# A fused vision block on one core: attention's value product on 64x32 tiles instead of 113x64 block-diagonal stationaries, and one filler left out

## The chip, the cores and the metric

The kernel runs on one core of a Trainium2 chip. The metric is the device time of one execution in microseconds, in float32 but for two small MLPs. Before: 3321.04 us, the median of three runs (3319.8 to 3326.78).

## The reference

The input x is 32 images of 56x56 tokens with 24 channels. Five layers follow each other; the change touches the first:

```python
# L0: shifted window attention, 7x7 windows, 3 heads of 8 channels, then an MLP
shifted = roll(x, (-3, -3)); win = window_partition(shifted)      # 32*64 windows of 49 tokens
h = layernorm(win); q, k, v = h @ wq, h @ wk, h @ wv              # 24 -> 3 heads x 8
attn = softmax(q @ k.T / sqrt(8) + mask)                          # per head, 49x49
out = (attn @ v).reshape(-1, 49, 24) @ wo + bo
t = x + window_reverse(out); t = t + gelu(layernorm(t) @ w1 + b1) @ w2 + b2
# L1: layernorm, 24 -> 48, 3x3 convolution back to 24, silu, residual
# L2, L3: per channel a Fourier mixer over the 3136 tokens, then an MLP in fp8, both with residuals
```

The value product is `attn @ v`; the change computes the same sums.

## The kernel before, in words

**Layout.** Four images are worked on together, a "quad": image j has its channels on partitions 32j to 32j+31 (24 channels, some constants), its tokens along the free axis. `for q in range(nq)` runs eight quads one after the other: window_attention, mlp, conv, then twice mixer and ffn. Each engine has its own program, written out by hand in this order; semaphores (`wait_ge`, `then_inc`) join them. All matrix products go through `mm` at L1128, so every one of them has that line in the profile, and is told apart by its tiles and shape. A float32 product is recorded as two passes, each a weight load (PEld) and a matmul (PE).

**Window attention** (L1213). A quad has 8 rows of 8 windows. One step n works on two windows of four images; there are 32 steps, four to a row of windows (t = n // 4, dw = n % 4). The loop is a software pipeline, and TensorE's queue in each iteration is:

- scores of the step 6 ahead (8 products, 32 partitions by 49 columns) and turned scores of this step (8 products). They wait for `maxed`, which VectorE's row maximum (L979) of the step before releases, and for `exped`, ScalarE's exponential (L741) of the step before.
- the value product of the step before (L1283 to L1291): for 2 windows, 3 heads and 2 pairs of images, one product of `ring` (stationary) and `pt` (moving). `ring` holds the values of a pair of images as a block diagonal: image 2g on partitions 64 to 112 in columns 0 to 31, image 2g+1 on partitions 0 to 48 in columns 32 to 63, and a column of ones by which the softmax sum comes out. The three heads are added up in bank 4 of PSUM. The last one releases `weighed`.
- at dw = 0 keys and queries (`wk`, `wq`) of two rows of windows ahead; at dw = 1 the sums spread over the channels (`spread`) with the centering of the second norm, then the values of the next row (`xh`, `wv`: 16 products, 128 partitions by 49 columns) and a transpose of the row maxima; at dw = 3 the output projection with the variance.

ScalarE copies keys (L755) and queries (L762, two halves) out of PSUM, takes exponentials (L741), squares and logarithms of the norms (L707, L719, L724) and the output (L747). VectorE takes maxima (L979), writes value blocks (L1009), multiplies keys and queries by head masks (L996, L1019), adds the residual (L987) and divides by the softmax sum (L1028).

**MLP** (L1353). `MLP_ORDER` starts with row 0, whose norm is ready. After its first product TensorE's queue has at i = 1 the filler `keep_busy(4, 1)` (L1359): one product of constants, 128x128 by 448 columns, into bank 4, whose result nobody reads. Then the last row's centering (L1363), its variance (L1365), and `keep_busy(5, 2)`; after that, rows 7, 1, 2 and so on. ScalarE loads the table of gelu (L794, 1.28 us) once its last root of the norm (L724) is done, and takes gelu of every half row; the convolution's first table load (L799) ends the stage for it. `keep_busy` stands in six other places, which stay.

**GpSimd** builds a table for the mixer before the first quad's part of it (L593 to L601, products and stores in turn), and only then zeroes borders and copies rows from `xw` to `xs` (L642), for which the convolution's centering waits.

Of the kernel before, what the change touches and what calls it, by code (L numbers as in the profile page):

```python
# [23 lines left out]
QI = 4  # L24
NQ = B // QI
RW = 32
WS, SHIFT, NH, DH = 7, 3, 3, 8
L = WS * WS
# [16 lines left out]
PADL = 64  # L45
STEPS = NW * NW // 2
SIDE = PADL + L
# [84 lines left out]
def ln_count(q, k):  # L132

    return q * LN_N + NW + k + 1
# [66 lines left out]
def down_bank(i):  # L201

    return 6 + (i + 1) % 2
# [61 lines left out]
def build_kernel(nc, x, keep, raw, g2, g4, out, nq=NQ):  # L265
    ctx = ExitStack()
    with ctx:
# [42 lines left out]
        ps = ctx.enter_context(nc.psum_tensor("ps", [128, 8, 512], F32))  # L310

        def K(name):
            at, n = KEEP_AT[name]
            return keep_sb[:, at:at + n]
# [7 lines left out]
        def part(area, at, *shape):  # L322
            n = int(np.prod(shape))
            v = area[:, at:at + n]
            if len(shape) == 2:
                v = v.rearrange("p (a b) -> p a b", b=shape[1])
            if len(shape) == 3:
                v = v.rearrange("p (a b c) -> p a b c", b=shape[1], c=shape[2])
            return v, at + n

        at = 0
        km, at = part(area_h, at, 2, NW, NH * L)
        qk, at = part(area_h, NTOK, 5, NW, PADL)
        qs, ks = qk[:, 0:2], qk[:, 2:5]
        mx, at = part(area_h, at, 2, 2 * NW * NH)
        mxt, at = part(area_h, at, 2, SIDE)
        assert at <= 2 * NTOK
        qm, at = part(area_t, 0, 3, NW, NH * L)
        pt, at = part(area_t, at, 2, 2, 6 * L)
        assert at <= HW * PAIR  # L340
        osb, at = part(area_y, 0, 2, TW)
        osn, at = part(area_y, at, 2, TW)
        lns, at = part(area_y, at, TW)
        rec, at = part(area_y, at, TW)
        assert at <= NTOK
        ring = area_z.rearrange("p (b u n) -> p b u n", b=2, n=NH * PADL)
# [11 lines left out]
        yc, at = [None, None], 0  # L358
# [15 lines left out]
        m29, at = part(area_t, 0, QI * CI)  # L374
        down, at = part(area_t, at, 2, 2 * RW)
        yy = area_h[:, 0:2 * NTOK].rearrange("p (g n) -> p g n", g=2)
        xq8 = area_t[:, 0:NTOK // 4].bitcast(F8)
        at = NTOK // 4
# [747 lines left out]
        def _(pe):  # L1126
            def mm(o, a, b, start=True, stop=True):
                return pe.matmul(o, a, b, start=start, stop=stop)  # L1128
# [9 lines left out]
            def crossed(bank, w, still, moving):  # L1138

                for o in range(0, 128, BLOCK):  # L1140
                    r = slice(o, o + BLOCK)
                    ins = mm(ps[BLOCK - o:2 * BLOCK - o, bank, 0:w], still[r, r], moving[r, :])
                return ins
# [24 lines left out]
            def keep_busy(bank, n):  # L1168

                for _ in range(n):  # L1170
                    mm(ps[:, bank, 0:TT], K("center"), keep_sb[:, 0:TT])
# [41 lines left out]
            def window_attention(q):  # L1213
# [25 lines left out]
                for n in range(-8, STEPS + 4):  # L1239
                    t, dw = n // 4, n % 4  # L1240
                    k = n + AHEAD
                    u = k // 4
# [31 lines left out]
                    k = n - 1  # L1274
                    if 0 <= k < STEPS:

                        u = k // 4
                        pe.wait_ge(exped, q * STEPS + k + 1)
                        if k % 4 == 0:
                            pe.wait_ge(v_kept, q * NW + u + 1)  # L1280
                            if u >= 1:
                                pe.wait_ge(out_kept, q * NW + u)
                        for i in range(2):  # L1283
                            w = 2 * (k % 4) + i
                            for h in range(NH):
                                for g in range(2):
                                    o = NH * L * i + L * h
                                    ins = mm(ps[PADL * g:PADL * g + PADL, 4, L * w:L * w + L],
                                             ring[0:SIDE, u % 2, 2 * w + g, PADL * h:PADL * h + PADL],
                                             pt[0:SIDE, k % 2, g, o:o + L], start=h == 0, stop=h == NH - 1)  # L1290
                        ins.then_inc(weighed, 1)  # L1291
                    if dw == 0 and 1 <= t + 2 < NW:

                        u = t + 2
# [10 lines left out]
                    if dw == 1 and 0 <= t - 1 < NW:  # L1305
# [5 lines left out]
                        if t - 2 >= 0:  # L1311
# [4 lines left out]
                            i = t - 2  # L1316
# [5 lines left out]
                    if dw == 1 and 0 <= t + 1 < NW:  # L1322

                        u = t + 1
                        pe.wait_ge(k_kept, q * NW + min(u + 2, NW))
                        for w in range(NW):
                            for jj in range(2):
                                far = PADL - PADL * jj
                                ins = mm(ps[far:far + L, 7, 2 * C * w:2 * C * w + 2 * C],
                                         xh[:, TW * u + L * w:TW * u + L * w + L], wv[:, jj, :])  # L1330
# [7 lines left out]
                    if dw == 3 and 0 <= t - 1 < NW:  # L1338
# [3 lines left out]
                        if t - 2 >= 0:  # L1342
                            k = LN_AT[LN_WIN2, t - 2]
# [9 lines left out]
            def mlp(q):  # L1353
                pe.wait_ge(w2_loaded, 16 * HC)
                for i in range(NW + 1):
                    if i < NW:
                        row = MLP_ORDER[i]
                        if i == 1:
                            keep_busy(4, 1)  # L1359
                            pe.wait_ge(attended, q * NW + NW)  # L1360
                            pe.wait_ge(logged, ln_count(q, LN_AT[LN_WIN2, NW - 2]))
                            k = LN_AT[LN_WIN2, NW - 1]
                            crossed(6, TW, K("center"), xw[:, TW * (NW - 1):TW * NW]).then_inc(centered, 1)  # L1363
                            pe.wait_ge(squared, ln_count(q, k))
                            crossed(6, TW, K("variance"), sq[:, k % 2, 0:TW]).then_inc(var_made, 1)  # L1365
                            keep_busy(5, 2)
                        pe.wait_ge(normed, ln_count(q, LN_AT[LN_WIN2, row]))
                        for p in range(2):
                            u = 2 * i + p
                            if u >= 3:  # L1370
                                pe.wait_ge(geglu, q * 2 * NW + u - 2)
                            pe.sem_inc(passed_pe, 1)
                            for jj in range(2):
                                r = slice(64 * p + RW * jj, 64 * p + RW * jj + RW)
                                ins = mm(ps[0:HID, 2 * (u % 3) + jj, 0:TW], w1[r, :],
                                         xh[r, TW * row:TW * row + TW])
                            ins.then_inc(up_made, 1)
                    if i >= 1:
                        i1 = i - 1
                        if i1 >= 2:  # L1380
                            pe.wait_ge(mlp_added, q * NW + i1 - 1)
                        pe.wait_ge(geglu, q * 2 * NW + 2 * i1 + 2)
                        pe.sem_inc(passed_pe, 1)
                        for j in range(QI):
                            ins = mm(ps[RW * j:RW * j + RW, down_bank(i1), 0:TW], w2[:, :],
                                     hid[0:HID, (2 * i1 + j // 2) % 4, j % 2, :])
                        ins.then_inc(down_made, 1)
# [265 lines left out]
            for q in range(nq):  # L1653
                window_attention(q)
                mlp(q)
                conv(q)
                for l in range(2):
                    mixer(q, l)
                    ffn(q, l)
# [168 lines left out]
```

## Time and profile before

| | |
|---|---|
| median of three runs | 3321.04 us |
| profiled execution, its own time | 3324.36 us |
| its span | 3322.6 us |
| mean granted TensorE clock | 0.971 of full |
| TensorE busy, weight loads busy | 87%, 55% |
| VectorE, ScalarE, GpSimd busy | 50%, 48%, 11% |
| chain of work that ended last | TensorE 69%, ScalarE 13%, VectorE 7%, issue 7% |

The span is the time from the first to the last instruction, the execution's own time is 1.8 us more. The chain of waits is followed back from the last instruction; "issue" is time in which an engine waited for nothing that the profile shows. Ends of matmuls are modelled, so the start of a matmul or of a weight load says more than its end. Times in the rows are microseconds from the start of the span.

### The profile page before, as it was taken

Reading aid. Unit: us, or ns where it says so; the run is one execution under the profiler, and the core shown is the slowest. Engines: PE = TensorE matmul, PEld = TensorE weight load, DVE = VectorE, ACT = ScalarE, POOL = GpSimd, SP = SyncE. Lnnn points to the kernel's source line nnn. Section 1 sums busy time; section 2 is a strip of 40 time slices with the busy share of each in tenths; the row PEclk is TensorE's granted clock in tenths of the full one; section 3 lists DMA queues with packets and bytes.
Section 4 is the critical chain, followed back from the end, with each engine's and each line's share of the span. In section 5 each row is a group of like instructions: output and inputs, shape, how many; then the busy total and the mean of one; then the engine's idle time right before and its main releaser. Section 6 shows DMA issues by size and latency. Waiting matters only on the chain.

```text
span 3322.6 us, 110007 instructions
## 1 busy us (share of the span) xinstructions
PE 2898.2 (87%) x49148; PEld 1838.1 (55%) x49148; DVE 1665.9 (50%) x2707; ACT 1611.3 (48%) x2899; POOL 363.6 (11%) x574
## 2 busy tenths in 40 slices
PE   6868889888899898998989989888898988988888
PEld 3536546466455573564744747447465474553754
DVE  5524546355553545544464445644457354572554
ACT  3542455533555425644266353563535535456245
POOL 4520010000100011001010011000110001100001
PEclk8989999999999999999999999999999999999999
DMA  2322000210001100110001100021000210001100
GB/s 80 69 59 52 2 16 5 53 33 2 17 16 50 25 2 17 32 51 6 2 18 42 46 1 2 18 54 34 1 2 19 54 34 1 2 19 34 33 1 16
DMA packets 28434, 84.79 MB, mean 26 GB/s; under 512 B 22002, under 2 KB 23138, under 8 KB 24114
## 3 DMA queue, kind: packets, MB, share of 16 engines
q1 hardware_dynamic: 26690, 72.55, 9.1%
q8 instruction: 395, 6.47, 0.8%
q0 software_dynamic: 1280, 5.21, 0.6%
q14 instruction: 69, 0.57, 0.1%
HBM read 61.70 MB, written 14.84 MB: 23 GB/s over the span
## 4 chain that ended last, share of the span: by engine, by line
PE 69%; ACT 13%; DVE 7%; issue 7%; SPq 3%; DMA 1%; ACTq 0%; DVEq 0%
PE ps L1128 69%; ACT lv L719 2%; SPq L495 2%; ACT area_ty L851 2%; ACT rs L724 2%; ACT sq L707 1%; DMA area_hz<-f_all 1%; DVE xs L1098 1%; DVE area_hz L979 1%; ACT area_hz L762 1%; ACT sq L705 1%; ACT area_ty L843 1%; DVE area_hz L996 1%; DVE area_ty L1094 1%; DVE area_ty L1070 1%
## 5 line engine op out<-in xcount | busy, mean ns | idle before, releaser
L1128 PE MATMUL ps<-area_hz 32*49 32x147 f32 (+3 forms) x7180 | 363.7, 288 | 89.2 <-DVE area_hz L979 24.1
L1128 PE MATMUL ps<-area_ty,area_hz 113*64 113x49 f32 (+2 forms) x10240 | 409.5, 256 | 8.8 <-ACT area_ty L741 8.1
L827 ACT ACTIVATE area_hz<-ps 121x384 f32<-121x384 f32 (+2 forms) x256 | 129.6, 519 | 583.5 <-PE ps L1128 583.5
L1128 PE MATMUL ps<-sq,keep_sb 64*64 64x392 f32 (+1 forms) x1728 | 340.2, 540 | 68.5 <-ACT sq L707 44.7
L1128 PEld LDWEIGHTS ps<-area_hz 32*49 32x49 f32 (+3 forms) x7180 | 290.2, 151 | 183.4 <-issue 160.9
L1128 PEld LDWEIGHTS ps<-area_ty,area_hz 113*64 113x64 f32 (+2 forms) x10240 | 319.4, 132 | 82.1 <-issue 80.9
L1128 PE MATMUL ps<-area_ty,g_sb 56*112 56x192 f32 (+1 forms) x3712 | 311.5, 321 | 26.0 <-DVE area_ty L1070 19.7
L1128 PEld LDWEIGHTS ps<-area_ty,g_sb 56*112 56x112 f32 x3712 | 293.0, 173 | 44.7 <-issue 44.0
L1128 PE MATMUL ps<-xs,keep_sb 64*64 64x448 f32 (+1 forms) x1184 | 217.2, 543 | 80.4 <-DVE xs L1098 49.7
L1070 DVE COPY area_ty<-ps 120x896 f32<-120x896 f32 (+1 forms) x192 | 164.8, 858 | 236.9 <-PE ps L1128 236.9
L719 ACT ACTIVATE lv<-ps 128x448 f32<-128x448 f32 (+1 forms) x304 | 158.6, 522 | 220.3 <-PE ps L1128 220.3
L979 DVE TENSOR_REDUCE area_hz<-ps 113x12 f32<-113x588 f32 x256 | 194.2, 763 | 140.0 <-PE ps L1128 140.0
L940 DVE TENSOR_TENSOR area_ty<-ps,rs 128x448 fp8e5<-128x448 f32 (+2 forms) x240 | 161.6, 673 | 195.7 <-ACT rs L724 195.7
L827 ACT ACTIVATE area_ty<-ps 120x896 f32<-120x896 f32 (+1 forms) x192 | 140.2, 730 | 243.8 <-PE ps L1128 243.8
L741 ACT ACTIVATE area_ty<-ps 113x588 f32<-113x588 f32 x256 | 168.3, 657 | 172.7 <-PE ps L1128 171.5
L617 POOL CAST area_ty<-area_ty 128x1344 fp8e5<-128x1344 f16 x112 | 146.2, 1305 | 866.2 <-DVE area_ty L1105 866.2
L724 ACT ACTIVATE rs<-lv 128x448 f32<-128x448 f32 (+2 forms) x368 | 223.7, 608 | 33.8 <-ACT lv L719 1.1
L1128 PEld LDWEIGHTS ps<-sq,keep_sb 64*64 64x64 f32 x1728 | 80.8, 133 | 270.6 <-ACT sq L707 136.4
L707 ACT ACTIVATE sq<-ps 128x448 f32<-128x448 f32 (+1 forms) x304 | 156.7, 534 | 140.8 <-PE ps L1128 139.1
L1128 PE MATMUL ps<-keep_sb,area_hz 112*58 112x56 f32 (+1 forms) x6144 | 192.5, 228 | 17.5 <-ACT area_hz L827 16.2
L1128 PEld LDWEIGHTS ps<-keep_sb,area_hz 112*58 112x58 f32 (+1 forms) x6144 | 190.2, 139 | 20.3 <-issue 20.1
L1081 DVE SCALAR_TENSOR_TENSOR xs<-ps,bn_bias,xs 128x448 f32<-128x448 f32 x112 | 76.6, 684 | 233.7 <-PE ps L1128 233.7
(124 smaller groups left out, 4325.7 us busy)
## 6 DMA issues: line engine op xcount, KB each, us to landing
area_hz<-f_all SPq DMA_DIRECT2D x16, 2541.0 KB
xw<-x_in SPq DMA_DIRECT2D x8, 1568.0 KB, 6.8
y_out<-xs SPq DMA_DIRECT2D x32, 252.0 KB
f_all<-piece POOLq DMA_DIRECT2D x16, 317.6 KB, 3.7
area_hz<-raw_in SPq DMA_DIRECT2D x1, 2894.0 KB, 9.4
g_sb<-g_in SPq DMA_DIRECT2D x6, 355.2 KB
area_ty<-area_hz SPq DMA_DIRECT2D x128, 9.2 KB
g_sb<-g_in SPq DMA_DIRECT2D x2, 710.5 KB
```

The lines of the kernel that those rows point to most:

```text
L495: sp.dma_start(g4_sb[r + HALF * g:r + HALF * (g + 1), :, g, :], g4[r:r + HALF, :, :]).then_inc(tables_loaded, 16)
L617: gp.tensor_copy(hq8[:, i % 2, :, :], r16, saturate=False).then_inc(f_hid, 1)
L707: act.activation(sq[:, k % 2, 0:w], ps[:, center_bank(k), 0:w], ACT.Square).then_inc(squared, 1)
L719: act.activation(lv[:, k % 2, 0:w], ps[:, variance_bank(k), 0:w], ACT.Ln).then_inc(logged, 1)
L724: act.activation(rs[:, k % 2, 0:w], lv[:, k % 2, 0:w], ACT.Exp, scale=-0.5).then_inc(root, 1)
L741: act.activation(pt[0:SIDE, n % 2, :, :], ps[0:SIDE, 2:4, 0:6 * L], ACT.Exp).then_inc(exped, 1)
L827: act.activation(dst, src, ACT.Relu if st in (ST_H, ST_F2) else ACT.Copy).then_inc(sc_kept, 1)
L940: ve.tensor_tensor(o, a, b, ALU.mult, **kw).then_inc(normed, 1)
L979: ve.tensor_reduce(mx[0:SIDE, u % 2, :].rearrange("p (g c r) -> p g c r", g=2, c=4)[:, :, k % 4], ps[0:SIDE, score_bank(k):score_bank(k) + ...
L1070: ins = ve.tensor_copy(dst, src)
L1081: ve.scalar_tensor_tensor(xs[:, sl], ps[:, 7, 0:TT], bn_bias[:, l:l + 1], xs[:, sl], ALU.add, ALU.add).then_inc(ve_kept, 1)
L1128: return pe.matmul(o, a, b, start=start, stop=stop)
```

## The change

The value product goes from 12 float32 products a step to 24: one for each of the four images, 49 partitions by 32 columns, in place of one for each pair, 113 by 64 with zeros off the diagonal. The loop over g becomes a loop over j with g = j // 2 and jj = j % 2. Image j takes its 49 partitions (from 64 for even j, from 0 for odd j) and its own 32 columns of `ring` and its rows of `pt`, and writes 32 partitions of PSUM bank 4. `ring`, `pt` and all other instructions stay. In the MLP `keep_busy(4, 1)` is left out.

```diff
--- before.py
+++ after.py
@@ -1283,11 +1283,13 @@
                         for i in range(2):
                             w = 2 * (k % 4) + i
                             for h in range(NH):
-                                for g in range(2):
-                                    o = NH * L * i + L * h
-                                    ins = mm(ps[PADL * g:PADL * g + PADL, 4, L * w:L * w + L],
-                                             ring[0:SIDE, u % 2, 2 * w + g, PADL * h:PADL * h + PADL],
-                                             pt[0:SIDE, k % 2, g, o:o + L], start=h == 0, stop=h == NH - 1)
+                                for j in range(QI):
+                                    g, jj = j // 2, j % 2
+                                    o, at = NH * L * i + L * h, PADL * h + RW * jj
+                                    r = slice(PADL - PADL * jj, PADL - PADL * jj + L)
+                                    ins = mm(ps[RW * j:RW * j + RW, 4, L * w:L * w + L],
+                                             ring[r, u % 2, 2 * w + g, at:at + RW],
+                                             pt[r, k % 2, g, o:o + L], start=h == 0, stop=h == NH - 1)
                         ins.then_inc(weighed, 1)
                     if dw == 0 and 1 <= t + 2 < NW:
 
@@ -1356,7 +1358,6 @@
                     if i < NW:
                         row = MLP_ORDER[i]
                         if i == 1:
-                            keep_busy(4, 1)
                             pe.wait_ge(attended, q * NW + NW)
                             pe.wait_ge(logged, ln_count(q, LN_AT[LN_WIN2, NW - 2]))
                             k = LN_AT[LN_WIN2, NW - 1]
```

## Rows read from the trace of the kernel before

**Rows 1.** The page, part 1: busy time, share of the span, instructions, per engine.

```profile
PE 2898.2 (87%) x49148; PEld 1838.1 (55%) x49148; DVE 1665.9 (50%) x2707; ACT 1611.3 (48%) x2899; POOL 363.6 (11%) x574
```

**Rows 2.** Groups of TensorE instructions by shape: busy us, mean ns, idle before.

```profile
L1128 PE MATMUL ps<-area_ty,area_hz 113*64 113x49 f32 x6144 | 235.2, 226 | 0.4 <-issue 0.3
```

**Rows 3.** Timeline, core 0: start us, us, engine, line, operation, count; product, values, scores.

```profile
531.77 0.30 PE L1128 MATMUL ps<-area_hz 32*49 32x147 f32 x4
...
531.89 0.30 PE L1128 MATMUL ps<-area_hz 32*49 32x147 f32 x4
...
532.15 0.78 PEld L1128 LDWEIGHTS ps<-area_ty,area_hz 113*64 113x64 f32 x24 [0.21 <-issue]
...
536.43 0.81 PEld L1128 LDWEIGHTS ps<-wv,area_ty 128*49 128x49 f32 x32 [0.61 <-issue]
```

**Rows 4.** Timeline of one row of windows (10.4 us): four products and their neighbours.

```profile
528.09 0.78 PEld L1128 LDWEIGHTS ps<-area_ty,area_hz 113*64 113x64 f32 x24 [0.22 <-issue]
...
528.20 0.77 DVE L979 TENSOR_REDUCE area_hz<-ps 113x12 f32<-113x588 f32 x1 [1.95 <-PE ps L1128]
...
529.09 0.16 PEld L1128 LDWEIGHTS ps<-area_hz 32*49 32x49 f32 x5 [0.22 <-issue]
...
529.80 0.78 PEld L1128 LDWEIGHTS ps<-area_ty,area_hz 113*64 113x64 f32 x24 [0.22 <-issue]
...
530.05 0.55 DVE L1028 TENSOR_TENSOR area_ty<-area_ty 128x392 f32<-128x392 f32 x1
...
530.66 0.13 PEld L1128 LDWEIGHTS ps<-area_ty,keep_sb 64*64 64x64 f32 x1
...
532.99 0.13 PEld L1128 LDWEIGHTS ps<-area_ty,wk 64*64 64x64 f32 x1
...
534.46 1.01 ACT L762 ACTIVATE area_hz<-ps 64x392 f32<-64x392 f32 x2
...
534.48 0.78 PEld L1128 LDWEIGHTS ps<-area_ty,area_hz 113*64 113x64 f32 x24 [0.22 <-issue]
...
535.58 0.13 PEld L1128 LDWEIGHTS ps<-area_ty,spread 64*64 64x64 f32 x1 [0.32 <-issue]
```

**Rows 5.** Timeline of the end of the stage, same four images.

```profile
574.88 0.78 PEld L1128 LDWEIGHTS ps<-area_ty,area_hz 113*64 113x64 f32 x24 [0.22 <-issue]
...
575.72 0.13 PEld L1128 LDWEIGHTS ps<-area_ty,spread 64*64 64x64 f32 x1
```

**Rows 6.** Timeline of TensorE in the convolution: the longest run of short loads.

```profile
621.70 10.29 PE L1128 MATMUL ps<-area_ty,wconv 32*32 32x392 f32 x370
```

**Rows 7.** Timeline of TensorE at the start of the MLP, first and second quad.

```profile
149.30 1.86 PE L1128 MATMUL ps<-keep_sb 128*128 128x448 f32 x2
...
151.09 1.33 PE L1128 MATMUL ps<-xw,keep_sb 64*64 64x392 f32 x4
...
588.66 1.15 PE L1128 MATMUL ps<-keep_sb 128*128 128x448 f32 x2
...
589.74 0.88 PE L1128 MATMUL ps<-xw,keep_sb 64*64 64x392 f32 x4
```

**Rows 8.** Windows: busy us (count) PE, PEld, DVE, ACT, POOL; clock, DMA share, GB/s.

```profile
585.60:588.90 3.30, 3.30 (x17) 0.93 (x18) 1.12 (x2) 1.03 (x2) 0.45 (x4) 0.50 0.19 39
...
1807.60:1814.20 6.60, 6.60 (x40) 1.64 (x40) 1.54 (x3) 3.46 (x5) 1.94 (x9) 0.50 0.71 153
```

**Rows 9.** Timeline of ScalarE: the table loads around two MLPs.

```profile
593.27 1.28 ACT L794 ACT_TABLE_LOAD   x1
...
608.38 1.28 ACT L799 ACT_TABLE_LOAD   x1
...
1803.75 1.28 ACT L794 ACT_TABLE_LOAD   x1
...
1821.72 1.28 ACT L799 ACT_TABLE_LOAD   x1
```

**Rows 10.** Timeline before the first convolution: what TensorE waited for.

```profile
192.01 3.04 PE L1128 MATMUL ps<-xs,keep_sb 64*64 64x392 f32 x16 [17.80 <-POOL xs L642]
```

## The prediction

> **What bounds the kernel.** The page comes first: TensorE is busy 87% of the span, VectorE 50% and ScalarE 48% [rows 1], so work taken off it may shorten the kernel, if it lies on the path. The groups by shape then say how much the changed product is: 6144 passes, 24 in each of 256 steps, busy for 235 us [rows 2]. That is a stock from which a saving is drawn, not a saving. What counts is read in the timeline of single steps [rows 3, 4]: how long one product takes, what limits it, and whether what follows starts as soon as it is done or waits for another engine. The same view at the MLP's start gives the filler [rows 7], the windows the granted clock there [rows 8].
>
> **What one product costs.** Its 24 weight loads run from 532.15 for 0.78 us [rows 3]. They run in pairs, one for each half of the columns, so in 12 rounds; the last load takes about 0.14, which leaves 0.64 us for 11 rounds, 58 ns each. The values (128x49, 48 columns moved) have 32 loads in 0.81 us, also in pairs: (0.81 - 0.13) / 15 = 45 ns a round [rows 3]. Both moved nearly as many columns (49 and 48), but loaded 64 and 49: the round of the old product goes with its load, 0.91 ns a column. Scores move 147 columns in rounds of 0.12 us (531.77 to 531.89) [rows 3], 0.82 ns a column moved, so 49 moved columns need some 41 to 46 ns. The new product has 48 passes, four to a round if the four images run at the same time: again 12 rounds, each loading 32 columns (some 30 ns by the load) and moving 49. So the load stops being the limit, the stream becomes it, and a round takes 46 ns. I expect 11 x 46 ns + 0.13 = 0.64 us for the loads, 0.14 us less than now. Bounds from both sides: by the load alone 30 ns a round, 0.46 us (0.32 less); by the supply of passes, from scores, where 8 passes begin in 0.12 us [rows 3], 15 ns each, 48 x 15 = 0.72 us (0.06 less); by the slowest supply in sight, the taps of the convolution, 10.29 / 370 = 28 ns each [rows 6], 1.33 us (0.55 more). I take 0.12 less: the stream, with a little given back where 32 passes of scores go ahead in the same queue. The taps are far from this (16 tiles at once, 392 columns moved), scores are the nearest.
>
> The skill's page "TensorE: Matmul & The Clock Gate" (section on the 56 ns gap) puts the least distance from one matmul's start to the next at about 25 ns however few columns it moves; by it the product would take 48 x 25 = 1.2 us. The 15 ns above speak against it.
>
> **What of it lies on the path.** One row of windows is four steps [rows 4].
> - First product: loads 528.09 to 528.87. The next scores begin at 529.09, after the row maximum (528.20 + 0.77 = 528.97), which started with the scores before. Gain 0; it could be about 0.16 us longer for nothing.
> - Second: ends 530.58. The projection begins at 530.66, when VectorE's division is done (530.05 + 0.55 = 530.60). Gain 0, and hardly any slack (0.02).
> - Third: 532.15 to 532.93, keys and queries at 532.99. Nothing else holds them, and the copies of ScalarE and all that follows hang on them. The whole gain passes.
> - Fourth: ends 535.26. The sums wait for ScalarE's second copy of the queries (534.46 + 1.01 = 535.47) until 535.58. Gain 0, slack 0.26.
>
> So one product in four pays. I went through the 32 of this quad in the same way: five like the third (511.98 to 552.96, one to a row of windows), one in the first row (514.31), and four of the last ten (565.31, 570.60, 574.88, 579.30), where the pipeline runs empty and one chain goes through product, projection and exponentials; there the loads end at 575.66 and the spread begins at 575.72 [rows 5]. Ten of 32: 10 x 0.12 = 1.2 us a quad. The first product of each quad, now followed without a change of tile shape by the values, I cost at nothing: what it saves the new change of shape takes back.
>
> **The filler.** From its start to that of the centering behind it are 1.79 us in the first quad and 1.08 in the second [rows 7]. Three quads (first, fifth, eighth) are of the first kind, five lie between 1.08 and 1.30, on average 1.19. Behind it nothing but TensorE is waited for: attention's last row has long been added, and the chain goes on through centering, square, variance and root to the gelu table. So its time is gained, less what the work moved forward loses at the lower clock: the clock is 0.50 (1.2 GHz) until 588.9 [rows 8], and the centering (0.88 at 2.4 GHz, 1.33 when mostly at 1.2 [rows 7]) now begins in it. Estimated loss 0.27 us in the five, 0.35 in the three (there it reaches the variance).
>
> **The first quad gives nothing.** TensorE waits 17.8 us before its first convolution for GpSimd's copy [rows 10], which comes after the table it builds; what attention and MLP save there only makes this wait longer. Seven quads count.
>
> **The sum.** Attention 7 x 1.2 = 8.4 us. Filler 2 x 1.79 + 5 x 1.19 = 9.5, less 5 x 0.27 + 2 x 0.35 = 2.0, so 7.5. Together 15.9 us: the profiled execution would go from 3324.4 to 3308.5. It stands 3.3 us above the median of the three runs; from the median, 3321.0 - 15.9 = 3305.1 us.
>
> **The rivals.**
> - A, the product gains nothing (12%): the supply of passes is the limit (0.72 us or a little more), and only the filler counts: 3321.0 - 7.5 = 3313.5, give or take 3. For it: 80 passes of scores and product now go through one queue in a step. Against: 15 ns a pass still fit.
> - B, slower (10%): the four images do not run at once. If images on the same partitions (0 and 2, 1 and 3) take turns, a round is 2 x 46 = 92 ns, the loads take 11 x 92 ns + 0.13 = 1.14 us, 0.36 more. Above the slacks of the four products that is 0.20 + 0.34 + 0.36 + 0.10 = 1.0 us a row of windows, 8 a quad, 56 in seven quads; less the filler +48.5, 3370. At the taps' 28 ns a pass it would be near 3410. It outweighs the filler once a product is some 0.1 us longer than now. Against it: scores of four images, two on a bank, are busy 0.30 us in all where one pass of theirs takes nearly that [rows 3]; for it: no row has two short products on the same 64 partitions in 32-column tiles.
> - C, the clock (14%): the changed quad is some 2 us shorter, so its idle moments fall otherwise against the instants at which the clock is regranted, and a filler less stands in them. Between the table loads one MLP takes 608.38 - 593.27 = 15.1 us, another 1821.72 - 1803.75 = 18.0 [rows 9]: in this one the clock is 0.50 from 1807.6 on [rows 8]. Three quads are of the long kind. If all eight were, five more would cost 5 x 2.9 = 14 us: 3319. If none were, 6 us less: 3299.
>
> The skill's page "TensorEngine Tiling (Array Packing)" (Restrictions and Gotchas, PSUM pressure) says that different row tiles cannot access the same PSUM bank at the same time. Here even images read partitions from 64, odd ones from 0, and all write bank 4; by that rule even and odd ones would take turns, at the price of B. Scores already write one bank from two row tiles, on other partitions, in one round, so the trace speaks against the rule in this form.
>
> **How the numbers follow.** The forecast has 64%, its own range 3298 to 3313: the product's 0.06 to 0.20 us for 70 products is 4 to 14 us, and the clock's instants move each quad by a little. With A, B and C the 8 in 10 are 3295 to 3322: left out are B and the edges of C. Something over 0.2% (6.6 us, about what a measurement can tell from no change) faster is below 3314.4: nearly all of the forecast, over half of A, a third of C, together 0.74. Within 0.2%: the rest of A, most of C, 0.15. Slower: B and an unfavourable C, 0.11.
>
> **What would show it.** Right: 48 loads of 49x32 in some 0.64 us a product; rounds of 46 ns; keys and queries 0.12 us sooner; the first, second and fourth product of a row followed by longer gaps at the same distance from the scores before; the row of windows 10.3 us instead of 10.4; one product of `keep_sb` less before the last row's centering; a longer wait for GpSimd in the first quad. Wrong: loads over 0.8 us, starts of the four images far apart, or more stretches at 0.50 in attention or MLP.

## The result and the profile after

The changed kernel takes 3396.18 us (median of 4 runs, 3386.77 to 3406.73), the kernel before beside it 3323.91 us: ratio 1.0218, 95% interval 1.0180 to 1.0256. It is 72 us slower where 16 us faster were forecast, and far outside the range. The profiled execution took 3386.77 us, its span is 3385.0 us, at a mean granted clock of 0.963 (0.971 before).

The page of the changed kernel, parts 1 and 3 (busy time and instructions of each engine; queues: packets, MB, share):

```profile
PE 2898.3 (86%) x55276; PEld 1814.0 (54%) x55276; DVE 1669.4 (49%) x2707; ACT 1616.7 (48%) x2899; POOL 366.4 (11%) x574
...
q8 instruction: 443, 7.26, 0.9%
```

The same queue of the kernel before:

```profile
q8 instruction: 395, 6.47, 0.8%
```

TensorE is busy for as long as before to 0.1 us (2898.2 us, [rows 1]) while the span has grown by 62 us: the time is in waiting, not in work. The other engines' work is also unchanged. What has grown is the number of TensorE's instructions, by 6128 weight loads and as many matmuls, and with them the queue that brings instructions: 48 packets of 16 KB more for 12,256 instructions more, so one packet carries about 255.

The new product by itself is what was predicted. Weight loads of one product in the timeline of the changed kernel (start, us, engine, line, operation, count; in brackets the idle time ahead):

```profile
530.83 0.59 PEld L1128 LDWEIGHTS ps<-area_ty,area_hz 49*32 49x32 f32 x48 [0.22 <-issue]
```

0.59 us for 48 loads, where the old one took 0.78 for 24 [rows 3]. But a few steps later the same product looks like this, same view:

```profile
544.30 0.35 PEld L1128 LDWEIGHTS ps<-area_ty,area_hz 49*32 49x32 f32 x25 [0.22 <-issue]
545.38 0.33 PEld L1128 LDWEIGHTS ps<-area_ty,area_hz 49*32 49x32 f32 x23 [0.73 <-issue]
```

After 25 of 48 loads none is under way for 0.73 us. No wait stands in the middle of a product, all operands are the step's own, and the profile puts the idle time down to "issue", for which it knows no cause. Such stops (idle time put down to "issue" between two matmuls of the same shape) stand in products and in scores alike; most of those in the second quad are 0.3 to 1.1 us long. In the attention of the last seven quads there are 82 of 0.15 us or more, 67 of them of 0.4 us or more, where the kernel before has one. Counted in TensorE's recorded instructions from the start, all 82 stand at number 193 or 194 modulo 256. And in the groups by shape, changed kernel:

```profile
L1128 PE MATMUL ps<-area_ty,area_hz 49*32 49x49 f32 x12288 | 209.5, 208 | 46.5 <-issue 45.8
...
L1128 PE MATMUL ps<-area_hz 32*49 32x147 f32 x3328 | 171.9, 308 | 48.9 <-DVE area_hz L979 32.1 <-issue 15.3 <-ACT area_ty L741 1.0
```

45.8 us of idle time inside the products where the old product had 0.3 [rows 2], and 15.3 in scores, which the change doesn't touch (in the kernel before issue is not among the three largest reasons listed for that group, the least of which has 0.9 us).

By stages: from the start of the first exponential (L741) to that of the last, attention takes 538.2 us in the kernel before, summed over the last seven quads (537.8 in the same kernel without the filler), and 591.8 us in the changed one. The second quad's first exponential starts 7.3 us later (509.56 against 502.24). Together these are 61 of the 62.4 us between the spans. So the first quad's product does count: attention is 7.2 us longer there, and TensorE's wait for GpSimd took up only a part. Same view as [rows 10], changed kernel:

```profile
195.45 3.06 PE L1128 MATMUL ps<-xs,keep_sb 64*64 64x392 f32 x16 [10.91 <-POOL xs L642]
```

### The profile page after: what moved, and what is told of

Its sections match the earlier page's. It is cut to its first block, busy times and chain, and to the rows that moved or that the text cites. A ratio compares the mean times of both kernels' runs of the same rounds, so it can differ in the third digit from the quotient of the medians.

```text
span 3385.0 us, 122263 instructions
## 1 busy us (share of the span) xinstructions
PE 2898.3 (86%) x55276; PEld 1814.0 (54%) x55276; DVE 1669.4 (49%) x2707; ACT 1616.7 (48%) x2899; POOL 366.4 (11%) x574
## 4 chain that ended last, share of the span: by engine, by line
PE 69%; ACT 11%; issue 8%; DVE 8%; SPq 3%; DMA 1%; ACTq 0%; DVEq 0%
PE ps L1128 69%; ACT area_ty L851 2%; SPq L495 2%; ACT lv L719 2%; ACT rs L724 2%; DVE area_hz L979 2%; DMA area_hz<-f_all 1%; ACT sq L707 1%; DVE xs L1098 1%; ACT sq L705 1%; DVE area_hz L1009 1%; ACT area_ty L843 1%; DVE area_hz L996 1%; DVE area_ty L1094 1%; DVE area_ty L1070 1%
## 5 line engine op out<-in xcount | busy, mean ns | idle before, releaser
L1128 PE MATMUL ps<-area_hz 32*49 32x147 f32 (+3 forms) x7180 | 378.8, 292 | 110.9 <-DVE area_hz L979 35.4
L1128 PE MATMUL ps<-area_ty,area_hz 49*32 49x49 f32 (+2 forms) x16384 | 397.0, 233 | 58.0 <-issue 48.3
L1128 PEld LDWEIGHTS ps<-area_ty,area_hz 49*32 49x32 f32 (+2 forms) x16384 | 281.5, 112 | 146.5 <-issue 145.7
L741 ACT ACTIVATE area_ty<-ps 113x588 f32<-113x588 f32 x256 | 168.8, 659 | 199.4 <-PE ps L1128 198.2
```

What stands on the lines that cost most here:

```text
L741: act.activation(pt[0:SIDE, n % 2, :, :], ps[0:SIDE, 2:4, 0:6 * L], ACT.Exp).then_inc(exped, 1)
```

## The experiments

Theory S: TensorE's instructions come in blocks of 256, a block can't come faster than some 3.5 to 4 us, and the changed attention uses them up faster. Theory T: something in the new tiles (two row tiles, four images on one bank, narrower loads). Theory C: the missing filler and the clock. All ratios are to the kernel before, run beside.

**Which half of the change.** The filler alone left out:

```diff
-                            keep_busy(4, 1)
```

> The kernel before with the one filler between attention and the gelu table left out, nothing else. Theory S (TensorE waits for its own next instructions, so the time lost is in the product's added instructions alone): about 3316 us, 7 to 8 us below before. Theory T (the tiles themselves): the same, since no tile changed. Theory C (the filler's absence drops the clock, and that is where the time went): 3324 us or more, with more stretches at 1.2 GHz than before.

Measured 3327.39 us, ratio 1.0004 (0.9993 to 1.0015): no change, neither the gain of S nor a loss. The time and the lower clock (0.9653) are those that C gave for this kernel, but the 70 us are not in it. Below it is taken up again.

The product alone changed, filler kept:

> The changed kernel with the filler put back. Theory S: 3396 us and the filler's 7 us, about 3403 us, with the same pauses of TensorE inside the products. Theory C: the time goes back to about 3324 us.

Measured 3399.58 us, ratio 1.0224 (1.0207 to 1.0241). The loss is the product's, whole. C has fallen as its cause.

**The tiles or the count.** One line of the new product:

```diff
-                                    r = slice(PADL - PADL * jj, PADL - PADL * jj + L)
+                                    r = slice(0, SIDE)
```

> The changed kernel, but each image's product reads 113 partitions by 32 columns in place of its own 49: as many matmuls and weight loads as the changed kernel (48 of each in a product of four images), all on one tile of rows. The output is that of the kernel, the other image's rows meeting zeros or not as they stand. Theory S (instruction supply): the same as the changed kernel, 3396 us give or take 10, with the same pauses about every 256 instructions of TensorE. Theory T (two tiles of rows, or the narrower loads, disturb one another): 3330 us or less.

Measured 3393.31 us, ratio 1.0204 (1.0177 to 1.0231), with the same picture; weight loads of two neighbouring products in its timeline:

```profile
531.59 0.60 PEld L1128 LDWEIGHTS ps<-area_ty,area_hz 113*32 113x32 f32 x48 [0.22 <-issue]
533.75 0.36 PEld L1128 LDWEIGHTS ps<-area_ty,area_hz 113*32 113x32 f32 x25 [0.22 <-issue]
534.61 0.33 PEld L1128 LDWEIGHTS ps<-area_ty,area_hz 113*32 113x32 f32 x23 [0.50 <-issue]
```

With all images on one row tile of 113 partitions the undisturbed product is as fast and the stops are there as before. Two row tiles are not the cause. The two kernels share 48 loads and 48 matmuls, but also loads of 32 columns and four images on one bank; what follows separates these.

**The dose.** The new product for one window of two, for three of four, and only where [rows 4, 5] show work waiting for it; the filler left out in all three:

```diff
+                                if i == 1:
...
+                                if i == 1 or k % 2 == 1:
...
+                                if k % 4 == 3 or k >= 26:
```

> The filler left out; of a pair's two windows the second (i = 1) takes the new product and the first keeps the 113x64 stationaries: half of the added instructions, about 670 of TensorE's in a row of windows where before has 574 and the changed kernel 766. Theory S (a rate that the supply can hold up to a limit): 3305 to 3325 us, few pauses, since 670 instructions need some 9.7 us at the rate that the changed kernel's stretches hold, below the 10.4 us that a row takes. Theory T, or any cost in proportion to the new products: half way between 3316 and 3396 us, about 3356 us.

> The filler left out; three of four windows with the new product, 718 instructions in a row of windows. Between one window of two (3337 us, 670 instructions) and the changed kernel (3396 us, 766). Theory S: at the 14 to 15 ns an instruction that the changed kernel's stretches hold, 718 need 10.1 to 10.8 us where a row has 10.4: 3345 to 3370 us, with pauses in part of the rows. A cost in proportion: 3327 us and three quarters of 70, about 3380 us.

> The filler left out, and the new product only in the twelve steps of a quad where the profile of before shows work waiting for it (every fourth step, and the last six): some 622 instructions of TensorE in a row of windows, against 574 and 766. Theory S (a limit on the instructions in a stretch, nothing below it): no cost; ten products by 0.12 us in seven quads are gained, 3327 less 8 is 3319 us, between 3312 and 3327. A cost in proportion to the new products: 12 of 32 by the 70 us that the changed kernel lost, 3353 us.

Measured: 3337.32 us, ratio 1.0038 (1.0023 to 1.0053); 3365.14 us, 1.0122 (1.0102 to 1.0142); 3319.75 us, 0.9988 (0.9976 to 1.0000). Half of the new products cost 10 us over the kernel without the filler, three quarters 38, all of them 69. The first missed its range by 12 us, of which the filler's gain that didn't come is 7; the other two fell in theirs. The proportional cost (3356, 3380, 3353) is out in the first and the third, and 15 us off in the second.

**The count elsewhere.** In both products' kernels the first window's scores and turned scores of each step left out (the exponential reads what stands in the bank), filler left out:

```diff
-                            if 0 <= k < STEPS:
+                            if 0 <= k < STEPS and i == 1:
                                 for ins in scores(score_bank(k), u, 2 * (k % 4) + i, NH * L * i,
...
-                            if 0 <= n < STEPS:
+                            if 0 <= n < STEPS and i == 1:
                                 for ins in turned_scores(t, 2 * dw + i, NH * L * i, L if n else PADL):
```

> The changed kernel, and of each step's two windows the first has its scores and its turned scores left out (the exponential reads what stands in the bank): 128 instructions of TensorE less in a row of windows, 638 in place of 766, products untouched. Together with the next kernel, which leaves out the same scores of the kernel with the old product (446 in place of 574). Theory S (what counts is the number of instructions in a stretch, wherever they come from): the two are within 10 us of each other, since both are below the some 700 that a row of 10 us can be supplied with. Theory T, or anything in the product itself: the new product still costs some 70 us more.

> The kernel before without the filler, and with the same half of the scores left out. Theory S: this one and the one above within 10 us of each other, both somewhat below 3327 us. Theory T: this one some 70 us below the one above.

Measured 3308.13 us (ratio 0.9950, 0.9931 to 0.9968) and 3276.76 us (0.9857, 0.9834 to 0.9879): 31 us apart. Neither expectation held. The new product costs less than half of what it costs with all scores, though it is untouched, so a fixed cost of the product, as T has it, doesn't fit; but neither does "within 10 us". By itself this is the weaker argument against T, since with fewer scores TensorE may also have more slack; what speaks more plainly is that the stops inside the untouched products become fewer. My bound was taken against a row of windows of 10 us, and without half of the scores a row is shorter (attention 506.9 in place of 537.8 us), so that fewer instructions still come at nearly the same rate. The groups of the first of the two show it:

```profile
L1128 PE MATMUL ps<-area_ty,area_hz 49*32 49x49 f32 x12288 | 211.3, 213 | 29.1 <-issue 28.0 <-ACT area_ty L747 0.6
```

28.0 us of issue in place of 45.8. Put together, over the last seven quads; "time per instruction" is attention's time with the old product and the same scores (537.8 or 506.9 us), by the number of TensorE's instructions recorded in the kernel's own attention:

| new product | instructions | time per instruction | attention, longer by |
|---|---|---|---|
| none | 28,476 | 18.9 ns | 0 |
| none, half of scores | 22,204 | 22.8 ns | 0 |
| 12 steps of 32 | 31,944 | 16.8 ns | 0.2 us |
| one window of two | 33,516 | 16.0 ns | 14.6 us |
| all, half of scores | 32,393 | 15.6 ns | 22.1 us |
| three of four | 36,036 | 14.9 ns | 39.3 us |
| all | 38,674 | 13.9 ns | 54.0 us |

Nothing down to 16.8 ns, then a steep rise: one curve for the doses and for the kernel whose instructions were taken away elsewhere. Each row is one profiled execution, and by the next experiment the place where blocks begin may count for some 12 us, so the curve is rough.

**Where the stops stand.** The changed kernel with 32 small float32 products ahead of attention:

> The changed kernel with 32 passes of 4 columns (64 instructions of TensorE) at its start, whose results nobody reads. Theory S, instructions that come in blocks of 256: the pauses stand at other places of the code, 64 instructions earlier in every row of windows, and the time stays within 10 us of the changed kernel's. If the pauses were made by what the instructions there do (a conflict of two tiles, a bank), they would stay at the same products and scores.

Measured 3410.38 us, ratio 1.0253 (1.0236 to 1.0271), 14 us above the changed kernel and so beyond the 10 us; its profiled execution has a clock of 0.960 against 0.963. Its attention takes 603.7 us in the last seven quads where the changed kernel's takes 591.8, with the same instructions, so where in the code a block begins seems to matter as well as how many there are (one profiled execution of each). A float32 product is two passes, so these were 128 instructions, not the 64 that I wrote: up to the first exponential the trace counts 682 in place of 554. The 71 stops of 0.15 us or more (53 of 0.4 or more) again stand at 193 or 194 modulo 256, so at other instructions of the code, 128 earlier. The stop of the changed kernel inside the product at 544.30 was ahead of numbers 17,089 and 17,090. The same two instructions are numbers 17,217 and 17,218 here, and their product runs through (551.37, last line). The stop is still ahead of number 17,089, which now lies in the products of keys and queries, which the change doesn't touch; timeline of the shifted kernel:

```profile
548.22 0.87 PE L1128 MATMUL ps<-area_ty,wk 64*64 64x392 f32 x2
549.88 0.54 PE L1128 MATMUL ps<-area_ty,wq 64*64 64x392 f32 x1 [0.80 <-issue]
...
551.37 0.59 PEld L1128 LDWEIGHTS ps<-area_ty,area_hz 49*32 49x32 f32 x48 [0.22 <-issue]
```

The places follow the count and not what the instructions do.

**The supply by itself.** Behind the last block of the kernel before, with nothing waiting for it:

```diff
+            pe.wait_ge(ffn_added, nq * 2 * NT)
+            for _ in range(504):
+                for g in range(2):
+                    mm(ps[PADL * g:PADL * g + PADL, 7, 0:L], keep_sb[0:SIDE, 0:PADL], keep_sb[0:SIDE, 128:128 + L])
+            for _ in range(252):
+                for j in range(QI):
+                    r = slice(PADL - PADL * (j % 2), PADL - PADL * (j % 2) + L)
+                    mm(ps[RW * j:RW * j + RW, 6, 0:L], keep_sb[r, 0:RW], keep_sb[r, 128:128 + L])
+            for _ in range(63):
+                for j in range(QI):
+                    for i in range(QI):
+                        r = slice(RW * i, RW * i + RW)
+                        mm(ps[RW * j:RW * j + RW, 2 + i, 0:4], keep_sb[r, 0:RW], keep_sb[r, 128:132])
```

> The kernel before, and behind its last block three streams of TensorE that nobody waits for, 1008 passes (2016 instructions) each: on 113 rows by 64 columns as in the old product, on 49 rows by 32 columns with two row tiles as in the new one, and on 32 by 32 in sixteen tiles with 4 columns moved. Results are read by nobody. By the tiles alone the three need 29 us (58 ns for 2 passes), 11.6 us (46 ns for 4) and at most that. Theory S: the second and the third both take 27 to 32 us, 13.5 to 16 ns an instruction, in pieces of 256 instructions with a stop between, and the first, which is just at that rate, about 29 us with few stops. Theory T: the second and third in 12 us.

Measured 3483.0 us, in a single run. Each stream has 1008 float32 products, and so 4032 instructions: all the times in the expectation, of both theories, are to be doubled. The windows of the three streams (busy us and count of PE, then of PEld; further on the clock and the DMA share), and one piece of each in the timeline:

```profile
3314.00:3371.00 57.00, 57.00 (x1998) 56.89 (x1995) 0.00 (x0) 0.00 (x0) 0.00 (x0) 1.00 0.02 4
3371.20:3426.50 55.30, 41.32 (x1920) 38.64 (x1920) 0.00 (x0) 0.00 (x0) 0.00 (x0) 0.53 0.02 4
3426.60:3481.00 54.40, 21.80 (x2040) 20.26 (x2039) 0.00 (x0) 0.00 (x0) 0.00 (x0) 0.50 0.02 5
```

```profile
3344.90 7.21 PEld L1128 LDWEIGHTS ps<-keep_sb 113*64 113x64 f32 x244
...
3371.22 1.45 PEld L1128 LDWEIGHTS ps<-keep_sb 49*32 49x32 f32 x128 [0.27 <-issue]
3374.96 2.65 PEld L1128 LDWEIGHTS ps<-keep_sb 49*32 49x32 f32 x128 [2.29 <-issue]
3385.37 2.65 PEld L1128 LDWEIGHTS ps<-keep_sb 49*32 49x32 f32 x128 [0.81 <-issue]
3388.84 2.66 PEld L1128 LDWEIGHTS ps<-keep_sb 49*32 49x32 f32 x128 [0.82 <-issue]
...
3430.04 1.25 PEld L1128 LDWEIGHTS ps<-keep_sb 32*32 32x32 f32 x128 [1.77 <-issue]
3433.51 1.26 PEld L1128 LDWEIGHTS ps<-keep_sb 32*32 32x32 f32 x128 [2.22 <-issue]
```

The old product's stream runs through without a stop: 57.0 of 57.0 us busy, 14.3 ns an instruction, which is its own work (58 ns for two passes). The other two run in pieces of exactly 128 loads and 128 matmuls, and the pieces start 3.47 to 4.02 us apart whether their work takes 1.3, 1.5 or 2.7 us: 13.6 to 15.7 ns an instruction. By their tiles alone the second needed 23 us, by the measured work of its pieces at the lower clock at most 42 (15.75 x 2.65); it took 55, and the third, with next to no work (1.3 us a piece), as long. In the queue of instructions there is one packet to a piece; from 3372 to 3481 on that queue:

```profile
q8 instruction: 31, 0.51, 1.9%
```

31 packets in 109 us. These two streams ran at the low clock of 1.2 GHz (0.53 and 0.50 in the windows). That the pace is not this clock's, the changed kernel shows in its second quad, where attention's stretch from 520 to 580 ran at 1.00 and its 15 packets still began 3.36 to 4.21 us apart, 3.8 on average:

```profile
520.00:580.00 60.00, 51.45 (x1970) 32.01 (x1966) 41.04 (x55) 35.80 (x69) 0.00 (x0) 1.00 0.03 6
```

Nor does the transfer itself fill the time. In the last two streams a packet begins 1.0 to 1.2 us (once 1.5) after the piece before it has begun, takes 0.9 to 1.5 us, and the next piece starts 2.3 to 2.9 us after the packet's start. So a piece and the next packet follow each other in turn, which adds up to the 3.5 to 4.0 us.

This is the limit behind the table above, seen with no other engine running. Attention before used a packet in 4.8 us on average (113 in 538.2 us), the changed one in 3.9 (151 in 591.8 us).

**Where the filler's gain went.** Two more kernels, one with the filler twice:

```diff
-                            keep_busy(4, 1)
+                            keep_busy(4, 2)
```

and the one with the new product in twelve steps, its filler kept:

> The kernel before with two passes of the filler in place of one. Each costs some 1.0 us a quad on the path to the gelu table, 7 to 8 us. If the clock is what a filler gives back: within 5 us of before, at a mean clock above 0.970. If the clock's change in the run without a filler was by chance of phase: 3331 us, clock 0.965 to 0.970.

> The new product only in every fourth step and the last six, as in the kernel that gave 3319.75 us, but with the filler kept. Leaving the filler out moved the time by nothing (its 7 us between attention and the gelu table came back as more half-clock time, 0.965 against 0.970), so: if the filler only holds the clock up, 3315 to 3322 us, the same as without it, at a mean clock nearer 0.970. If it is the new products that lowered the clock, 3323 us or more.

Measured 3328.54 us, ratio 1.0013 (0.9997 to 1.0029), and 3329.71 us, 1.0027 (1.0011 to 1.0042). Two fillers cost some 4 us, not to be told from nothing. That meets the first branch in words (within 5 us, clock 0.9708), but the kernel before beside it had 0.9703, so it shows no clock given back. The second kernel missed its 3315 to 3322 and came out as its other branch had it (3323 or more, clock 0.9677 over 12 runs). In the kernel without the filler the path is shorter just as forecast: in its second quad gelu's table loads start 1.0 us earlier (593.27, [rows 9]), and over the last seven quads the part from the last exponential to that load is 6.8 us shorter.

```profile
592.26 1.28 ACT L794 ACT_TABLE_LOAD   x1
...
1404.34 1.28 ACT L794 ACT_TABLE_LOAD   x1
...
1423.88 1.28 ACT L799 ACT_TABLE_LOAD   x1
```

But the MLP of the fourth quad now takes 1423.88 - 1404.34 = 19.5 us where the kernel before has 1417.22 - 1402.11 = 15.1. Timeline of the kernel before there, and a window over the same MLP:

```profile
1402.11 1.28 ACT L794 ACT_TABLE_LOAD   x1
...
1417.22 1.28 ACT L799 ACT_TABLE_LOAD   x1
```

```profile
1402.10:1417.20 15.10, 13.82 (x114) 4.05 (x112) 4.71 (x8) 13.43 (x17) 5.11 (x21) 1.00 0.57 123
```

A window over it in the kernel without the filler:

```profile
1404.30:1423.90 19.60, 17.96 (x114) 4.21 (x112) 4.95 (x8) 13.47 (x19) 5.09 (x21) 0.74 0.46 99
```

A clock of 0.74 where it was 1.00. Over the last seven quads the MLPs between these two loads take 116.2 us in place of 111.5. Over all its runs the mean granted clock is 0.9653 (10 runs) against 0.9701 (13 of the kernel before). In the runs of the kernel before alone, 0.01 of clock goes with 16 to 22 us, so 0.0048 would be 8 to 10 us, at least what the filler's absence gave. That is an estimate from how time and clock go together, and no run holds the clock fixed. Whether it holds for a filler in general stays open: the second one brought no clock (0.9708 against 0.9703 in 12 and 26 runs).

## Why the prediction was wrong

- **The product's cost**, "11 x 46 ns + 0.13 = 0.64 us": right, and a little better, 0.59 to 0.60 us where no stop falls into it. The rounds of its matmuls are 46 ns as forecast (the first of 48 starts 0.53 us before the last), those of its loads 42 ns. The old one took 0.78.
- **The step that failed** is the supply of instructions, asked for one product in a burst, "by the supply of passes, from scores, where 8 passes begin in 0.12 us, 15 ns each, 48 x 15 = 0.72 us", and then put at nothing in the sum. 15 ns is the pace within a block that is already there, and the 48 passes even start in 0.53 us. But a whole row of windows has some 574 instructions in 10.4 us before, 18 ns each, and would have 766 after, 13.6 ns each. The streams with little work run at 13.6 to 15.7 ns, attention is disturbed from 16 on, and the 192 added instructions a row, costed at nothing, cost 54 us in seven quads.
- **The taps.** The bound that I had in hand and dismissed, "the slowest supply in sight, the taps of the convolution, 10.29 / 370 = 28 ns each", has the right number, 14 ns an instruction, but by luck. In the kernel before, taps that follow each other start 25 ns apart on average also where no block begins, and in the run of [rows 6] the one stop at a block's beginning is 0.35 us long, ahead of 629.53 (number 193 modulo 256). So the taps go mostly at a pace of their own, which lies near that of the supply.
- **"One product in four pays"**: attention of the kernel with the new product in twelve steps is as long as before (538.0 against 538.2 us), so the 8.4 us didn't show. It has some stops of its own (9 of 0.15 us or more in seven quads, 1 before). What each gained product gives is not separated from this.
- **The filler, 7.5 us**: 6.8 us by the stages, and lost again, by all signs through the clock. Rival C priced just this (3299 to 3319 with both gains), but I gave it as a chance beside the forecast; no gain of a few microseconds stands in this kernel without the clock being looked at.
- **"The first quad gives nothing"**: for a gain. A loss of 7.3 us passed, since TensorE's wait for GpSimd could take up only a part: the copy itself came later, the wait went from 17.80 to 10.91 us, and the convolution began 3.4 us later (195.45 against 192.01, [rows 10]); another 3.9 us were lost on the way to the next quad.
- **Rival A** (supply, 3313.5) named the mechanism at the price of a burst. **Rival B** had the price, "At the taps' 28 ns a pass it would be near 3410", but under the mechanism of images that take turns, which the runs exclude: undisturbed products are at full speed, with one row tile or two. That its price came near the 3396 us measured is luck, as said of the taps.
- **The 25 ns from start to start** of the Trainium skill's page "TensorE: Matmul & The Clock Gate" did not decide: the 48 passes of a product start in 0.53 us. But the page "Runtime: NRT & Kernel Launch" of the Trainium skill (section on instruction fetch mechanics) has the rule that I didn't weigh: an engine's instructions are streamed in blocks of 16 KiB, 256 of them, by a DMA queue of its own. The trace agrees (16 KB a packet, stops 256 apart). The section also says that the cost of a boundary is mostly hidden, because issuing is slower than filling. Here that is so at 18.9 ns an instruction and not at 13.9.

The time is accounted for: 54 us in the attention of seven quads, 7 up to the second quad. What is not settled: why a block of the changed kernel comes once in 3.9 us on average rather than 3.5, why attention took 12 us longer with the blocks beginning elsewhere, and a few microseconds between neighbouring kernels. The version in twelve steps gave 0.9988 without the filler and 1.0027 with it, where the filler made no difference on the old product. So no version that beats the kernel before is shown.

## What to carry to other kernels

Before splitting a product into more, smaller ones, count TensorE's instructions (loads and matmuls, float32 twice) over the stage and divide the stage's time by them. Here nothing was lost at 16.8 ns each, 15 us at 16.0 and 54 us at 13.9, whatever a single product did in the timeline. To bound a supply, look at the densest stretch of several hundred instructions, not at the fastest burst; it shows a rate that the supply reaches, and whether it holds more takes a stream with little work. A product with zeros in its stationary may be the cheaper one because it takes half the instructions.

## What the runs showed that was not expected

- Idle time put down to "issue" in the middle of a group, at a fixed place modulo 256 in TensorE's instructions, is a late block of instructions. At worst in the changed kernel it is 3.9 us at once, in the first quad after 148 us; the kernel before has one as long in its first quad, ending at 247.7. What makes these two so long was not tested.
- With little work in the way, a block comes every 3.47 to 4.02 us (13.6 to 15.7 ns an instruction), in those streams each transfer begins only after the block before has begun. Attention is disturbed above this already, from about 16 ns on average; that its instructions come unevenly is the likely reason, not tested.
- A round of the four images' products is 46 ns on one row tile of 113 partitions and on two of 49. The values, which load 49 columns, have 45 ns [rows 3], so the load of 32 columns is not what sets it.
- A filler of 1 us per quad taken from the path left the time unchanged within 0.15%, the mean clock going from 0.9701 to 0.9653.
